# Second scan: the next batch's projections and convolution inside the chunk steps of the current one

## What is computed

```python
# per batch b: projection, causal convolution over 4 tokens, silu
proj = x @ in_proj_w.T                    # gate z (512), x|B|C (768), dt (64 heads)
xBC  = silu(conv(xBC)); xs, B, C = split(xBC)
dA   = dt * A                             # A per head
# per chunk: decay matrix, product within the chunk, state, product with the state
Lmat   = exp(segsum(dA))
Y_diag = einsum('bcthn,bcshn,bhcts,bcshp->bcthp', C, B, Lmat, xs)
states = einsum('bcshn,bhcs,bcshp->bchpn', B, decay, xs)   # carried from chunk to chunk
Y_off  = einsum('bcthn,bchpn,bhct->bcthp', C, prev, exp(dA_cum))
y = norm((Y_diag + Y_off + D * xs) * silu(z)) @ out_proj_w.T
# experts of the layer: 16 experts, 2 per token, gathered in tiles of 128 rows
h = silu(x @ w1.T) * (x @ w3.T);  out += (h @ w2.T) * weight
```

## Time and profile before

| | |
|---|---|
| median of 3 runs | 1279.89 us (1278.6 to 1288.63) |
| profiled execution | 1287.56 us |
| its span, first to last instruction | 1285.8 us |
| mean granted TensorE clock | 0.91 of full speed |
| TensorE busy | 1031.7 us (80%) |
| VectorE busy | 920.5 us (72%) |
| ScalarE busy | 490.4 us (38%) |
| GpSimd busy | 464.0 us (36%) |

### The profile page before, as it was taken

The page is one execution under the profiler, slowest core; times in us unless marked ns, Lnnn a source line. Parts: engine busy times, 40 slices in busy tenths (PEclk is TensorE's granted clock), DMA queues, the critical chain, the costliest instruction groups (busy, mean ns, idle before and its releaser), DMA issues.

```text
span 1285.8 us, 18516 instructions
## 1 busy us (share of the span) xinstructions
PE 1031.7 (80%) x6024; PEld 601.5 (47%) x6024; DVE 920.5 (72%) x1506; ACT 490.4 (38%) x1114; POOL 464.0 (36%) x333
## 2 busy tenths in 40 slices
PE   3988997878788878765677779997999889996885
PEld 2355455445445444434333535554555545563443
DVE  4767768898988888896487566666666656657585
ACT  2100235555445444440221154435443454335332
POOL 0000104778788888860540104232322223321000
PEclk9988999899898888877798889998989989989798
DMA  6940434878887888887800325342444335441121
GB/s 228 372 112 0 133 70 119 143 138 142 152 147 139 154 145 151 138 137 197 164 5 0 62 67 136 92 109 65 106 102 93 80 76 114 107 98 13 24 72 51
DMA packets 111186, 143.24 MB, mean 111 GB/s; under 512 B 30022, under 2 KB 97334, under 8 KB 110902
## 3 DMA queue, kind: packets, MB, share of 16 engines
q0 software_dynamic: 34464, 77.92, 33.5%
q1 hardware_dynamic: 76630, 64.14, 18.0%
HBM read 72.80 MB, written 39.46 MB: 87 GB/s over the span
## 4 chain that ended last, share of the span: by engine, by line
PE 29%; DVE 12%; DMA 7%; issue 3%; ACT 3%; SPq 2%; POOL 1%; ACTq 0%; DVEq 0%; POOLq 0%
PE bank L1418 4%; PE bank L1425 4%; PE bank L1851 3%; PE bank L1890 3%; DVE cv L2079 3%; PE bank L1834 3%; DMA sum<-yo,to_i 2%; PE bank L1843 2%; DMA crow<-cp_d 2%; PE bank L1876 1%; DMA x<-sum 1%; PE bank L698 1%; PE bank L686 1%; PE bank L1406 1%; PE bank L1907 1%
## 5 line engine op out<-in xcount | busy, mean ns | idle before, releaser
L1491 POOL DMA_INDIRECT sum<-yo,to_i x48 | 76.7, 1598 | 329.1 <-ACT yo L1445 318.7
L1164 POOL DMA_INDIRECT sum<-yo,to_i x80 | 156.9, 1962 | 44.8 <-issue 40.7
L1171 POOL DMA_INDIRECT xg<-xn_d,token_i x80 | 100.9, 1262 | 175.6 <-DVE to_i L460 93.5
L1011 PE MATMUL bank<-areaA,xgT 128*128 x320 | 130.5, 536 | 15.0 <-issue 9.4
L1028 PE MATMUL bank<-areaA,hidT 88*128 x320 | 97.7, 431 | 39.9 <-ACT hidT L1076 30.5
L2021 DVE TENSOR_TENSOR areaD<-areaD,gb 128x512 f32<-128x512 f32 x128 | 87.5, 689 | 30.4 <-ACT areaD L1977 21.4
L1977 ACT ACTIVATE areaD<-bank 128x512 f32<-128x512 f32 x128 | 76.0, 594 | 61.4 <-PE bank L1843 58.3
L1144 DVE TENSOR_TENSOR_SCAN xnT<-areaB,xnT 128x1024 f32<-128x1024 f32 x42 | 96.3, 2294 | 3.3
L1028 PEld LDWEIGHTS bank<-areaA,hidT 88*128 88x128 f32 x320 | 58.4, 203 | 75.2 <-issue 69.9
L1011 PEld LDWEIGHTS bank<-areaA,xgT 128*128 128x128 f32 x320 | 62.4, 213 | 60.7 <-issue 44.8
L686 PE MATMUL bank<-xnT,areaB 128*128 128x512 f32 x192 | 86.8, 599 | 0.8 <-DVE y L716 0.8
(11 more groups left out here) (335 smaller groups left out, 2149.8 us busy)
## 6 DMA issues: line engine op xcount, KB each, us to landing
y<-xnT POOLq DMA_DIRECT2D x21, 1024.0 KB
wst<-gu_f SPq DMA_DIRECT2D x96, 176.0 KB
y<-areaB POOLq DMA_DIRECT2D x11, 1024.0 KB
wst<-down_f SPq DMA_DIRECT2D x48, 176.0 KB
areaA<-in_gu SPq DMA_DIRECT2D x2, 2816.0 KB
gu_f<-in_gu POOLq DMA_DIRECT2D x1, 5632.0 KB, 18.6
sum<-yo SPq DMA_DIRECT2D x2, 2176.0 KB, 16.3
down_f<-in_down POOLq DMA_DIRECT2D x1, 2816.0 KB, 24.1
```

Of the source, the lines that this page charges most:

```text
L1011: last = nc.tensor.matmul(bank[:, GB + q % 2, 0:2 * FI], xgT[:, q % 2, k, :], wgu0_of(e, k), start=(k == 0), stop=(k == KD - 1))
L1164: nc.gpsimd.indirect_dma_start(sum0_d[q % 2], bass.IndirectOffsetOnAxis(ap=to_i[:, q:q + 1], axis=0), yo[:, q % 5, :], None, compute_op=AL ...
L1171: nc.gpsimd.indirect_dma_start(xg[:, q % 5, :], None, xn_d[0], bass.IndirectOffsetOnAxis(ap=token_i[:, q:q + 1], axis=0)).then_inc(s.gathe ...
```

## The change

There is one loop over all 32 chunks (and one step more to end the last), instead of a loop over batches with projections and steps. Only batch 0 is projected ahead of it. The ten projections of batch b + 1 stand in the steps of batch b, one in every third group (`proj_at`), the convolution one group later on VectorE, the tanh two and the silu three groups later. What they write (xb, xB, xC, gz) has two sets. The ninth step of a batch is gone: its last chunk is ended in the next batch's step 0. Expert parts go at 8 for 7 ticks, so that they end in step 5 of batch 3. `norm` stands in step 3 of the batch after, in group 1; mean_square and add_scan1 in groups 0 and 3. `crow_of` stands at group 1 and waits for products instead of S. The expert sums of all batches are loaded at the end, each into memory that is free by then, and added in the tail.

```diff
-        rows1 = sb("rows1", [P, PAIRS, D], F32, c1)
+        rows1 = [z.rearrange("p (t d) -> p t d", d=D) for z in (xb[:, 0, 0:2, :].rearrange("p g t -> p (g t)"), xb[:, 0, 2:4, :].rearrange("p g t -> p (g t)"),
...
-        LATE = 3
-        TICKS = NPROJ + (CH + 1) * G1
-        PIECES = []
...
-                    PIECES.append((b, "out", (step - 4) // 2))
+        CHUNKS = NB * CH
+        PARTS = 3 * (NT1 + 1)
+        PIECES = [(0, "proj", n) for n in range(NPROJ)]
+        for n in range(CHUNKS + 1):
+            b, step = divmod(n, CH)
+            if n < CHUNKS:
+                PIECES.append((b, "gb", step))
+            for g in range(G1):
+                if n < CHUNKS:
+                    PIECES.append((b, "seg", step, g))
+                if b + 1 < NB and (step * G1 + g) % 3 == 1 and (step * G1 + g) // 3 < NPROJ:
+                    PIECES.append((b + 1, "proj", (step * G1 + g) // 3))
+            if n % 2 == 0 and n > 2:
+                PIECES.append(((n - 4) // 2 // PAIRS, "out", (n - 4) // 2 % PAIRS))
         PIECES.append((NB - 1, "out", PAIRS - 1))
         AT = {name: n for n, name in enumerate(PIECES)}
...
+        def proj_at(n, g, late):
+
+            b, step = divmod(n, CH)
+            m, left = divmod(step * G1 + g - 1 - late, 3)
+            return m if b + 1 < NB and left == 0 and 0 <= m < NPROJ else None
+
+        def parts_of(tick):
+
+            return range(min(tick * 8 // 7, PARTS), min((tick + 1) * 8 // 7, PARTS))
...
+            def crow_of(n):
+
+                b, kk = divmod(n, CH)
+                if n > 1:
+                    sp.wait_ge(m_ready, group(b, kk, 0) - G1 + 1)
                 for r in range(3):
...
+            for n in range(CHUNKS + 1):
+                b, step = divmod(n, CH)
+                for g in range(G1):
+                    for m in parts_at(n, g):
+                        expert_sync(sp, m)
+                    if g == 1 and 0 < n < CHUNKS - 1:
+                        crow_of(n + 1)
...
+                                                        start=(old % 2 == 0 and g == 0 and u == 0), stop=False)
+                        last.then_inc(m_used, 1)
+                    m = proj_at(n, g, 0)
+                    if m is not None:
+                        project(b + 1, m)
+                    for part in parts_at(n, g):
+                        expert_tensor(pe, part)
+                if n % 2 == 0 and n:
+                    pair = (n - 2) // 2
...
+                    if step != 1 and n:
+                        state_of(act, b, max(step - 1, 0))
+                    nc.scalar.activation(gb[:, step % 2, :], o[:, 0:Q + P], ACT.Copy).then_inc(free, 1)
+                if n % 2 == 0 and n > 2:
+                    squares((n - 4) // 2 // PAIRS, (n - 4) // 2 % PAIRS)
+                for g in range(G1):
+                    if n < CHUNKS:
+                        o, free = take(act, b, "seg", step, g)
+                        if group(b, step, g) >= 2:
+                            act.wait_ge(m_ready, group(b, step, g) - 1)
+                        nc.scalar.activation(ex[:, g % 2, :], o, ACT.Exp).then_inc(free, 1)
+                    m = proj_at(n, g, 2)
+                    if m is not None and m < 6:
+                        tanh_of(b + 1, m)
+                    m = proj_at(n, g, 0)
+                    if m is not None:
+                        projected(b + 1, m)
+                    if n < CHUNKS and n > CH and step == 3 and g == 1:
                         norm(b - 1)
-                for step in range(CH + 1):
-                    if step < CH:
...
+                        products(b, step, g)
+                    m = proj_at(n, g, 3)
+                    if m is not None and m < 6:
+                        silu_of(b + 1, m)
+                    m = proj_at(n, g, 1)
+                    if m is not None and m < 6:
+                        convolve(b + 1, m)
+                    if m is not None and m >= 6 and g:
+                        gate_silu(b + 1, m - 6)
+                    if g == 2 and n % 2 == 0 and n > 2:
...
+                    if g == 1 and n < CHUNKS and step > 1:
+                        if step == 2:
+                            v.wait_ge(dec_in[b % 2], 16 * (b // 2 + 1))
                         v.wait_ge(yo_full, b * (CH - 1) + old)
-                        nc.vector.tensor_tensor(ys[half, :].rearrange("p (h d) -> p h d", d=HD), bank[half, CS, :].rearrange("p (h d) -> p h d", d=HD),
-                                                ecn[half, t, b, :, :].rearrange("p n h -> p (n h)").unsqueeze(2).to_broadcast([half.stop - half.start, HEADS, HD]),
-                                                ALU.mult).then_inc(y_tok, 1)
...
+            gated(NB - 1, PAIRS - 1)
+            gate(NB - 1, PAIRS - 1)
+            add_experts(0)
             sum_squares(NB - 1, PAIRS - 1)
+            add_experts(1)
             mean_square(NB - 1)
+            add_experts(2)
             add_scan1(NB - 1)
             add_experts(NB - 1)
```

425 lines of the change are left out of this document (193 added, 232 removed).

## The result

The changed kernel takes 1269.8 us (four runs, 1268.1 to 1271.1) against 1284.2 us of the kernel before (four runs beside it, 1278.6 to 1288.6): a ratio of 0.988 [0.984, 0.992]. It is faster by 1.2%; 1251 us had been forecast, in a range of 1216 to 1281. So the direction held and about half of the forecast gain of 28.9 us came. The profiled execution of after took 1271.14 us, 16.4 less than that of before, where the working had 28.5.

The account below looks back on a forecast made before the run. TensorE's idle and slow clock were to bound the kernel: 87.0 us beyond a 403.4 us floor in the steps. Added terms sum to 58.5, saving 28.5: 1259.1 profiled, less 7.7 for the median, about 1251 us, range 1216 to 1281.

Parts of the forecast that it names:

- item 6: In the chunk steps, gate projections hold ring banks until VectorE frees them one group later: 12 times 0.3, 3.6 us.
- The first projection stretch: Batch 0's projections ahead of the chunk steps, 737 to 773 us, were to stay within 1 us.
- (a): Removal of TensorE's 27.9 us idle in the three projection stretches between batches, by interleaving segments and products.
- (b): Removal of TensorE's 9.2 us crow wait by issuing the next chunk's loads at group 1.
- Item 3: Previous batch's norm on ScalarE in chunk step 3 delays S and the CS matmul: 12.4 us.
- Item 4: Doubled expert parts in one group, 17 times; tile end followed by next start counted free: 8 us.
- Item 5: Convolution's round trip over VectorE and ScalarE in the steps, 18 convolutions at 0.5 each: 9 us.
- Items 2 and 7: S and sq_sum waits in the last two steps, 3.5 us; slow clock in the steps, 12 us.
- Items 1, 4 and 5: Small waits on hidT, hid and issue, 10 us; doubled parts, 8 us; convolution's round trip, 9 us.
- B: Rival: the hid stalls return as waits on S and hid in the steps; 1278 us, chance 0.18.
- C: Rival: TensorE pays 3 us for each of 18 convolutions, so the kernel is slower; 1296 us, chance 0.06.
- D: Rival: ring turnover holds TensorE's clock at 0.84 in the steps; 1316 us, chance 0.03.

Follow-up runs that it names:

- h2: Changed kernel, gate product and expert copies earlier, first doubled part at group head, norm in group 2, add_scan1 in step 4: 1237.6 us, ratio 0.973.
- e4: Changed kernel with the crow loads back at group 2 behind the update of S: 1280.0 us, ratio 1.002 to the kernel before.
- g4: Kernel before with only the crow loads moved to group 1 behind the products of the chunk before: 1263.6 us, ratio 0.990.
- g4_again: Second run of the kernel before with only the early crow loads: 1262.2 us, ratio 0.993 to the kernel before.
- after_third: Changed kernel run unchanged for the third time: 1258.2 us, ratio 0.988 to the kernel before.
- e2: Changed kernel with VectorE's gate product at the head of its group, ahead of expert and segment products: 1252.1 us, ratio 0.983.
- e1: Changed kernel with one expert part for each of batch 0's ten projections again: 1258.9 us, ratio 0.985.
- e5: Changed kernel with ScalarE's expert copies ahead of the tanh and norm in each group: 1257.8 us, ratio 0.980.
- e6: Changed kernel with two of three convolution tap passes left out in batches 1 to 3: 1256.9 us, ratio 0.980.
- g1: Changed kernel with the first of two doubled expert parts at the head of its group: 1259.2 us, ratio 0.988.

## Why the prediction was right in direction and too large in size

Two terms of the sum failed. The gate's projections in the ring of two banks (item 6) were priced at 3.6 us and cost 8.1 us of direct waits, some 7 us of the time. The first projection stretch, which was to stay within 1 us, grew by 3.9. Beyond these, the forecast took its start from a profile of the kernel before that was longer than its twin. One by one:

- **The floor**, 403.4 us of TensorE's own work at full clock: right within a per cent. h2 shows 403.3 at 0.99.
- **What it removes.** (a) The 28.4 us for hid went, as said. (b) Crow went, as said, and it was worth more than its 9.2 us: alone it gives 10 to 13 us. e4, g4 and g4_again show that this was nearly the whole of the measured gain.
- **The base.** The sum was made against a profile with 490.3 us in the steps; its twin has 481.1. Against the mean of the two, 4.6 us were never there to be won; two profiles are few for such a mean. For the profiled execution the forecast was 1259.1; the three of after took 1271.1, 1263.6 and 1259.5, beside medians of 1284.2, 1283.2 and 1274.1 of the kernel before. The 7.7 us taken off for the median came with the high profile of before, and the changed kernel's own profiles lie only 1.3, -0.7 and 1.4 us above their medians.
- **Item 6, the gate's projections** in the ring: the term that failed in the steps. It was priced at 12 times 0.3, with one VectorE pass of 0.7 as the upper bound, 8. It is 8.1 us of direct waits in after, 6.3 in after_third (2.8 + 2.1 + 1.4), and some 7 us in the time. The bound was drawn from the pass itself; what sits before the gate's product in VectorE's queue, an expert product that itself waits for ScalarE, was left out. e2, which takes it away, shows this cause.
- **The first projection stretch**, "stays within 1 us": failed. 39.4 instead of 35.5. The 11 parts were counted, but not that two of them fell into one tick there, with a longer wait and a slow projection behind it; e1 brings back 35.4. The tail stayed, as said: 21.99 us, 22.45 before.
- **Item 3, the norm**, 12.4 us: the size was near (9.0 us of direct waits), the victim was another. The working led the delay through VectorE's products to S and the CS matmul; TensorE meets it earlier, at the expert copies behind the norm on ScalarE. S, which was to rise to 15, fell to 4.8. The hops between engines, put at 0.2 us there, are 0.04 and 0.05 in the rows of 1057 to 1058 us above. On the loads themselves: they block ScalarE for 2.9 us, from 947.24 to 950.16, so the 5.7 us that the prediction estimates from the Trainium skill, "ScalarE: Activation LUTs", section What ACT_TABLE_LOAD costs, are not seen in the changed kernel either.
- **Item 4**, 8 us for doubled parts, kind 2 to 0 "free": not free. At 790.2 us TensorE has waited 1.51 for yo, since part 0 needs what part 2's copy frees, and that copy stood behind a tanh; the wait is gone in e5, e6 and g1 alike. The total was not separated; avoiding doubling showed no gain.
- **Item 5**, the convolution's round trip, 9 us: two of the three passes are worth 7.5 us, so the term was a little small, if anything. The way was in half the one told: a tanh waits for the convolution and keeps the expert copies behind it. The other half of what e6 gave back are waits for S, sq_sum and hid behind VectorE.
- **Items 2 and 7** held: in the last batch's steps 0.83 us for sq_sum and 2.0 for S against 3.5 together, and 15.0, 13.8 and 12.6 us of slow clock in the three profiles (busy less 403.4) against 12.
- **Items 1, 4 and 5** can only be read together: of the 50.6 us idle in after, 28.9 are left when item 2's 2.8, the norm's 9.0, the gate's 8.1 and crow's 1.8 are taken off, against 10 + 8 + 9 = 27.

The account: the steps were to take 403.4 + 58.5 = 461.9 us. They take 469.0, 467.9 and 461.6, in the mean 466.2, 4.3 too long. The front costs 3.9, and the base 4.6. That makes 12.8 of the 13.5 us by which the ratio missed (28.9 us forecast against 1.2% of 1280, 15.4). That it comes so near is chance, with profiles that differ by 7 to 9 us. For the scored kernel's own profile it needs no mean: 1271.1 against 1259.1 are 12.0 us, of which the steps have 7.1 (4.1 idle, 3.0 slow clock), the front 3.9 and all that comes ahead of it 1.4, less 0.4 in the tail.

That the direction held was owed to the crow loads, a small and separable piece of the change. Of the rivals, B ("the stalls only move") describes the interleaving by itself, since 4 us are left of it and no less idle time than in g4_again; it was given 0.18. It was wrong on where: hidT, yo and the gate's banks, not S and hid. Why hidT's small waits of 0.2 to 1.4 us, some 12 us in after, are more than the 4.1 before was not found. C would have needed 3 us for each convolution, and D a clock of 0.84; the steps ran at 0.96. The rule of the Trainium skill named with D, "TensorE: Matmul & The Clock Gate", section A second HAM failure mode: psum-queue depth-cycling, is not borne out here: the same ring stands in h2's steps at 0.99.

## What to carry to other kernels

Work that is interleaved into a loop joins the in-order queues of the loop's engines: price it by what stands before and behind it in each queue, that is, which instruction waits for an input not yet there, and whose bank or copy is behind it. Put what frees a bank or feeds TensorE ahead of what can wait (here two reorderings gave some 17 us, more than the interleaving itself), and before crediting a large change with its gain, run its smallest piece alone on the kernel before. Compare a forecast with several profiles of the kernel before, since one can be off by as much as the gain that is looked for.
